# A graph layer with mixing and experts on one core: the change of phases written as one table of steps

## The chip, the cores and the metric

One core of a Trainium2 chip runs the whole program in one launch. TensorE (PE) multiplies matrices, VectorE (DVE), ScalarE (ACT) and GpSimd (POOL) do the rest, and SyncE (SP) issues most DMAs. Each engine works through its own queue in order and waits on semaphores. The metric is the device time of one execution in microseconds; before the change it is 1598.66 us, the median of 3 runs (1596.49 to 1599.17).

## The reference

6250 nodes with 256 features, 100,000 edges sorted by target, 16 relations, all in float32:

```python
xn = layernorm(x)
transformed = einsum('ni,rio->rno', xn, W_rel)          # 16 relations
gnn = segment_sum(transformed[rel, src] * norm, dst)    # 100,000 edges
q, k, v = split(xn @ Wqkv)                              # 8 heads of 32
context = einsum('bnhd,bnhv->bhdv', softmax(k, over nodes), v)
gate = sigmoid(gelu((xn*ln_g + ln_b) @ Wg1 + bg1) @ Wg2 + bg2)
x = x + gnn + ((q @ context) * gate) @ Wproj + bproj
t = layernorm(x)                                        # experts
out = t + sum over the two best of 8 experts e: weight_e * (gelu(t @ w1[e] + b1[e]) @ w2[e] + b2[e])
return x + out
```

## The kernel before

The 6250 nodes lie in 49 row tiles of 128. **The first phase** (to about 720 us) takes tile by tile: it normalises, multiplies with the 16 relation matrices and stores the result as a `table` in HBM (four stores of a quarter each per tile), stores keys and normalised rows (`kv_d`), transposed rows and gate values, and from tile 24 on also gathers and sums the edges whose messages are already in the table. A product of two float32 matrices is made of three products of rounded halves (a high and a low part, `three`, L1826); a product in full float32 ("whole") is one instruction pair of twice the length.

**The second phase** takes pairs of row tiles, `i` = 0 to 23. Each pair has 8 edge groups, `S = 8 i + s`, alternately of three and two tiles of 128 edges: GpSimd gathers the rows of the table (`gathers`, L818, a ring of six groups), ScalarE scales them (`MSGS`), VectorE makes the selection matrix (`SELECT`) and, for split sums, the low part (`MSGS`), TensorE sums (`SUMS`) and VectorE adds the sum to the rows (`adds`). Groups of the pairs below `WHOLE` = 2 (S = 0 to 15) are summed whole, without low parts, the others in split halves. Then a pair goes through the mixer (`OUT`, `GATES`, `GATE`, `PROJ`), its second normalisation (`STATS`, GpSimd's `roots2`, `MEAN`, `NORM`, `TURN`), the choice of experts (`LOGIT`, `TOP`, `COMB`) and eight experts (`LAYER1`, `LOW`, `LAYER2`, `ADD`). In the loop three pairs overlap: the edges of pair i, the mixer of pair i-1, the experts of pair i-2, in the order of `SLOTS_OF_PAIR`, eight slots to a pair.

**Between the phases** the contexts of the mixer have to be finished. The keys of the first 24 tiles have been summed against a first maximum; the last four tiles are still in SBUF (`kvs`); the 21 tiles between come back from `kv_d` in six parts of 4 and 3 (`load_rows`, then `shifts` on VectorE, `exps` on ScalarE, `contexts` on TensorE). SyncE loads them after the last table store, then the first pair's rows (`load_pair`), then the expert weights in four chunks of 2 x 512 KB (`load_chunk(4)` to `(7)`), each of which ScalarE and VectorE split into high and low halves of the whole chunk (`split_hi`, `split_lo`). The later parts of the returned rows (256.5 KB for a tile) lie where the weights of chunks 6 and 7 go, so those two are split after the contexts; the third chunk is loaded when the first is split. GpSimd starts the gathers when the last table store has landed. At that point it also makes the head mask (`heads`, in `ctxbd`).

The order of these steps beside pairs 0 and 1 comes from three places: the tuple `SLOTS_OF_SECOND`, the constants below, and conditions in each engine's `slot_of`:

```python
PARTS_OF_SLOT = {0: (0, 1), 1: (2,), 2: (3,), 3: (4,), 4: (5,)}
SPLITS = ((0, 4), (0, 5), (1, 0), (1, 1))
SPLITS_LOW = ((0, 5), (0, 6), (1, 1), (1, 3))
```

On GpSimd the roots of pair 0 stand before the sixth group of pair 1 (`FIRST_ROOTS`), those of other pairs before the last gather of the next pair (`ROOTS`). VectorE, TensorE and GpSimd have a branch for edges that sum outside their window (`far`), which these inputs don't take.

## Time and profile before

| what | us |
|---|---|
| median of the runs | 1598.66 |
| the profiled execution | 1598.54 |
| its span | 1596.7 |
| PE busy in the span | 1563.8 (98%) |
| DVE busy | 1339.1 (84%) |
| ACT busy | 962.8 (60%) |
| POOL busy | 1021.2 (64%) |

The busy time of an engine is the time in which at least one of its instructions ran; for PE that is generous, since matmuls are pipelined and their ends are modelled. The granted clock is TensorE's, as a share of 2.4 GHz: 1.00 is that level, 0.50 the level of 1.2 GHz. A timeline row has the start, the duration from the first start to the last end of the instructions merged in it, the engine, the line, and in brackets how long the engine had been idle and what released it. SPq is the queue in which SyncE issues DMAs.

### The profile page before, as it was taken

How to read it: one execution, taken by the hardware profiler on the slowest of the kernel's cores; microseconds unless marked ns; L12 is line 12 of the kernel's file. 1: busy time of each engine (PE TensorE's matmuls, PEld its weight loads, DVE VectorE, ACT ScalarE, POOL GpSimd, SP SyncE). 2: the span in 40 equal slices, each digit the busy share in tenths (PEclk: the TensorE clock that was granted, in tenths of full speed). 3: DMA queues.
4: the chain of work that ended last, by engine and by line, in shares of the span. 5: the costliest groups of instructions: out<-in, count | busy, mean ns of one | idle time of the engine just before them, and what ended most of it. 6: DMA issues, size and time to landing. Idle time of an engine off the chain costs nothing.

```text
span 1596.7 us, 31746 instructions
## 1 busy us (share of the span) xinstructions
PE 1563.8 (98%) x10509; PEld 1439.2 (90%) x10509; DVE 1339.1 (84%) x3389; ACT 962.8 (60%) x2156; POOL 1021.2 (64%) x1111
## 2 busy tenths in 40 slices
PE   7999999999999999998799999999999999999998
PEld 6888788888888888887699999999999999999998
DVE  7888656488888888884699999999999999999985
ACT  4455322356565665654677776777677777777764
POOL 4433222677777777757687777777777777767720
PEclk9999999999999999999999999999999999999999
DMA  9776665688888889889433333343333333333320
GB/s 301 264 256 242 243 237 226 231 291 272 277 278 279 283 283 284 277 261 317 144 111 108 116 109 108 112 113 104 103 117 107 110 106 109 112 105 113 107 53 10
DMA packets 127076, 290.50 MB, mean 182 GB/s; under 512 B 21271, under 2 KB 49724, under 8 KB 126914
## 3 DMA queue, kind: packets, MB, share of 16 engines
q1 hardware_dynamic: 86068, 177.19, 30.2%
q0 software_dynamic: 39952, 110.13, 26.3%
q8 instruction: 85, 1.39, 0.4%
q10 hardware_dynamic: 894, 1.16, 0.2%
q14 instruction: 77, 0.63, 0.1%
HBM read 149.49 MB, written 138.90 MB: 181 GB/s over the span
## 4 chain that ended last, share of the span: by engine, by line
PE 94%; DMA 1%; DVE 1%; issue 1%; ACT 1%; POOL 1%; ACTq 0%; SPq 0%; DVEq 0%; POOLq 0%
PE bank L1826 74%; PE bank L2030 4%; PE bank L2031 3%; PE bank L1870 2%; PE bank L1871 2%; PE bank L1982 1%; PE bank L1881 1%; PE bank L2026 1%; POOL raw L700 1%; DMA raw<-table,idxa 1%; PE bank L2068 1%; PE bank L2080 1%; PE bank L1836 1%; DMA pad<-in_L_mix_Wg 1%; PE bank L2077 1%
## 5 line engine op out<-in xcount | busy, mean ns | idle before, releaser
L818 POOL DMA_INDIRECT stg<-table,idxcur x495 | 546.7, 1104 | 145.1 <-issue 133.1
L1826 PE MATMUL bank<-wreg,xt 128*128 128x512 f32 x2352 | 579.1, 397 | 0.2
L1826 PEld LDWEIGHTS bank<-wreg,xt 128*128 128x128 f32 x2352 | 433.4, 189 | 88.0 <-ACT stg L864 1.0
L700 POOL DMA_INDIRECT raw<-table,idxa x297 | 306.6, 1032 | 87.7 <-issue 73.7
L1826 PE MATMUL bank<-tt,wreg 128*128 128x256 f32 (+1 forms) x2400 | 324.4, 284 | 0.0
L1826 PE MATMUL bank<-wreg,ht 128*128 128x256 f32 x2352 | 313.1, 282 | 0.2 <-DVE ht L1727 0.2
L1826 PEld LDWEIGHTS bank<-tt,wreg 128*128 128x128 f32 x2400 | 300.4, 189 | 2.5
L1826 PEld LDWEIGHTS bank<-wreg,ht 128*128 128x128 f32 x2352 | 292.1, 189 | 0.4 <-DVE ht L1727 0.4
L1090 ACT ACTIVATE raw<-bank,cols 128x256 f32<-128x256 f32 (+1 forms) x400 | 164.8, 463 | 101.4 <-PE bank L1826 101.0
L1611 DVE SCALAR_TENSOR_TENSOR ml<-stg,nrm,mh 128x256 fp32r<-128x256 f32 x455 | 195.2, 478 | 13.0 <-ACT mh L1034 13.0
L1034 ACT ACTIVATE mh<-stg,nrm 128x256 fp32r<-128x256 f32 x455 | 200.8, 499 | 0.0
L889 ACT ACTIVATE mh_a<-raw,nrm 128x256 fp32r<-128x256 f32 x297 | 129.6, 500 | 118.1 <-DMA raw<-table,idxa 117.8
L1228 DVE COPY stg<-bank 128x512 f32<-128x512 f32 x196 | 134.2, 686 | 75.5 <-PE bank L1826 74.5
L1741 DVE SCALAR_TENSOR_TENSOR xres<-bank,raw,xres 128x256 f32<-128x256 f32 x392 | 169.7, 473 | 13.1 <-PE bank L1826 11.4
L864 ACT COPY stg<-bank 128x512 f32<-128x512 f32 x196 | 112.5, 581 | 101.8 <-PE bank L1826 100.2
L1361 DVE SCALAR_TENSOR_TENSOR ml_a<-raw,nrm,mh_a 128x256 fp32r<-128x256 f32 x297 | 126.7, 480 | 53.0 <-ACT mh_a L889 52.5
L1095 ACT CAST ht<-raw 128x512 fp32r<-128x512 f32 (+1 forms) x200 | 122.5, 612 | 72.4 <-PE bank L1826 67.4
L1727 DVE TENSOR_TENSOR ht<-raw,ht 128x512 fp32r<-128x512 f32 (+1 forms) x200 | 134.6, 673 | 11.7 <-ACT ht L1095 9.5
L2030 PE MATMUL bank<-mh,sel 128*128 128x256 f32 x455 | 120.3, 291 | 0.0
L2031 PE MATMUL bank<-ml,sel 128*128 128x256 f32 x455 | 117.0, 281 | 0.0
L665 POOL TENSOR_TENSOR xres<-xres,bpb 128x256 f32<-128x256 f32 x24 | 19.4, 809 | 136.0 <-DVE kvs L1215 135.5
L1594 DVE TENSOR_TENSOR sel<-dbl,dpr 128x384 fp32r<-128x384 f32 x198 | 95.0, 480 | 9.7 <-PE bank L2026 9.6
(244 smaller groups left out, 2134.8 us busy)
## 6 DMA issues: line engine op xcount, KB each, us to landing
table<-stg SPq DMA_DIRECT2D x196, 512.0 KB, 3.9
kv_d<-kvs SPq DMA_DIRECT2D x49, 256.5 KB, 5.2
xt_d<-xt SPq DMA_DIRECT2D x49, 256.0 KB, 4.7
xtp<-xt_d SPq DMA_DIRECT2D x24, 512.0 KB
stg<-table,idxcur POOLq DMA_INDIRECT x495
sk<-kv_d SPq DMA_DIRECT2D x24, 256.5 KB, 5.7
out_x<-xres SPq DMA_DIRECT2D x24, 256.0 KB
xres<-in_x POOLq DMA_DIRECT2D x23, 256.0 KB, 4.2
```

The lines of the kernel that those rows point to most:

```text
L700: pool.indirect_dma_start(ring_a[:, r * EARLY + j, :], None, table[0:LIMIT, :], bass.IndirectOffsetOnAxis(ap=idxa[:, at:at + 1], axis=0)). ...
L818: pool.indirect_dma_start(stg[:, ring_at(S, j), :], None, table, bass.IndirectOffsetOnAxis(ap=idxcur[:, at:at + 1], axis=0)).then_inc(gath ...
L889: act.activation(mh_a[:, (r % 2) * EARLY + j, :], ring_a[:, r * EARLY + j, :], ACT.Copy, scale=nrm[:, bass.ds(EB * q + j, 1)]).then_inc(hi ...
L1034: act.activation(mh[:, (s % 2) * CUT + j, :], stg[:, ring_at(S, j), :], ACT.Copy, scale=nrm[:, bass.ds(at + j, 1)]).then_inc(msg_hi, 1)
L1090: act.activation(hf[e % 2][:, c * 256:c * 256 + nt * P], bank[2 + e % 2][:, c * 256:c * 256 + nt * P], ACT.Gelu, bias=b1c[:, 2 * e + c:2 * ...
L1228: dve.tensor_copy(stage[:, j // 2, (j % 2) * 512:(j % 2 + 1) * 512], bank[3 + j % 4][:]).then_inc(copied(k, j)[0], 1)
L1611: dve.scalar_tensor_tensor(out=ml[:, m, :], in0=stg[:, ring_at(S, j), :], scalar=nrm[:, bass.ds(at + j, 1)], in1=halves(mh[:, m, :]), op0= ...
L1727: dve.tensor_tensor(ht[e % 2][:, LO, :, 0:n], cols2(hf[e % 2], n), halves(ht[e % 2][:, HI, :, 0:n]), ALU.subtract).then_inc(h_lo, 1)
L1741: dve.scalar_tensor_tensor(out=xk, in0=bank[6 + e % 2][:, a * C:(a + 1) * C], scalar=comb[:, a, e:e + 1], in1=xk, op0=ALU.mult, op1=ALU.ad ...
L1826: mm = pe.matmul(dst, stat(a, c), mov(b, c), start=(n == 0), stop=(n == 3 * chunks - 1))
L2030: pe.matmul(bank[u % 2][:, 0:C], sel[:, m, :], mh[:, m, :], start=(s % 2 == 0 and j == 0), stop=False)
L2031: mm = pe.matmul(bank[u % 2][:, 0:C], sel[:, m, :], ml[:, m, :], start=False, stop=(s % 2 == 1 and j == PART[1] - 1))
```

## The change

All steps of the pairs 0, 1 and 2 and of the change of phases stand in one tuple, `CHANGE`, in the order in which they are to run; each engine follows it and takes the entries that are its own (`follow`). `run` starts the loop with pair 3. `SLOTS_OF_PAIR` is unchanged but for a new name: the second half of `NORM` is now `KEEP` and stands right behind it. In the table `KEEP` stands later. The other parts:

- SyncE loads five of the returned rows (`FREE_ROWS`) in the last tile, right behind the store of the second quarter of its table rows, instead of behind the last quarter. The shifts and exponentials of the first two parts stand before the branch on far edges.
- TensorE's branch on far edges stands behind the first two parts of rows.
- The whole groups are S = 4 to 19 (`WHOLE_GROUPS`), not 0 to 15.
- The four expert chunks are split in halves (`HIGH n h`, `LOW_PART n h`), most of them behind the contexts; the splits are counted half by half (`splits_of`).
- The head mask is a `[P, 4]` tile made in the setup; the step `HEADS` reads it broadcast.
- The Gelu table is loaded in a step of its own (`GELU_TABLE`), before the contexts.
- The roots of pair 0 stand before the fifth group of pair 1, those of pair 1 before a gather of the sixth group of pair 2 (`EARLIER_ROOTS`). The second copy of indices of pair 0 stands between its gathers.
- Gelu's output and the choice of experts have buffers of their own (`hf`, `mix`), no longer in `raw`.

```diff
-    ROOTS, FIRST_ROOTS = (7, 1), (5, 0)
+    ROOTS, EARLIER_ROOTS = (7, 1), {1: (4, 0), 2: (5, 1)}
+    FREE_ROWS = 5
...
+        hf = [cd[:], wv[:].rearrange("p c n -> p (c n)")]
+        def whole(S):
+            return WHOLE_GROUPS[0] <= S < WHOLE_GROUPS[1]
+        def splits_of(n, h):
+            return 4 + 2 * (n - 4) + h + 1
...
+                    if at(k, NT - 1) and h == 1:
+                        sp.wait_ge(sum_a, ER)
+                        for b2 in range(2):
+                            sp.wait_ge(kv_st[b2], 16 * ((KEPT + SLOTS) // 2))
+                        for n in range(FREE_ROWS):
+                            load_row(n // 4, n)
...
+            sp.wait_ge(ctx1_mm, KEPT)
+            for n in range(FREE_ROWS, SLOTS):
+                load_row(1, n)
             first_phase_over(sp)
...
             for n in range(4, 6):
-                sp.wait_ge(w_lo, n + 1)
+                sp.wait_ge(w_lo, splits_of(n, 1))
                 load_chunk(n + 2)
...
+            def HIGH(n, h):
+                act.wait_ge(raw_in[n % 2], 32 * (n // 2 - 1))
+                if n >= 6:
                     act.wait_ge(ctx_mm, HELD + REST)
+                act.copy(wreg[:, HI, place_of(n), h * CC // 2].rearrange("p r o -> p (r o)"),
+                         raw[:, n % 2, h * WC * C:(h + 1) * WC * C]).then_inc(w_hi, 1)
+            def GELU_TABLE():
+                act.activation(small[0:1, 156:157], small[0:1, 157:158], ACT.Gelu)
             held_exps()
+            for ready in range(2):
+                EXP(ready)
             first_phase_over(act)
...
+            def LOW_PART(n, h):
+                dve.wait_ge(w_hi, splits_of(n, h))
+                dve.tensor_tensor(wreg[:, LO, place_of(n), h * CC // 2].rearrange("p r o -> p (r o)"),
+                                  raw[:, n % 2, h * WC * C:(h + 1) * WC * C],
+                                  halves(wreg[:, HI, place_of(n), h * CC // 2].rearrange("p r o -> p (r o)")),
                                   ALU.subtract).then_inc(w_lo, 1)
...
+            for ready in range(2):
+                SHIFT(ready)
+            dve.wait_ge(flag_ready, 1)
+            far = dve.value_load(flag[0:1, 0:1], min_val=0, max_val=NT * P * R)
+            first_phase_over(dve)
...
+WHOLE_GROUPS = (4, 20)
+CHANGE = (
+    "HELD_ROWS", "ROWS_OF 0", "ROWS_OF 1", "FAR_EDGES", "SELECT 0 0", "SELECT 0 1", "FADE", "SHIFT 2", "EXP 2", "SHIFT 3",
+    "MSGS 0 0", "ROWS_OF 2", "EXP 3", "SUMS 0 0", "ROWS_OF 3", "SHIFT 4", "MSGS 0 1", "EXP 4", "SELECT 0 2",
+    "ROWS_OF 4", "SUMS 0 1", "SHIFT 5", "EXP 5", "SELECT 0 3", "MSGS 0 2", "ADDS 0 0", "ROWS_OF 5", "MSGS 0 3", "GELU_TABLE",
+    "SUMS 0 2", "SUMS 0 3",
+    "CONTEXT", "SELECT 0 4", "MSGS 0 4", "SELECT 0 5", "CONTEXT_PE", "CONTEXT_TURN", "SUMS 0 4", "HIGH 4 0", "MSGS 0 5",
+    "VALUES", "ADDS 0 1", "LOW_PART 4 0", "HEADS", "SUMS 0 5", "HIGH 4 1", "HIGH 5 0", "SELECT 0 6", "QUERY", "GATES 0 2",
+    "LOW_PART 4 1", "QUERY_ROWS", "GATE_ACT 0 2", "OUT 0 2", "MSGS 0 6", "SELECT 0 7", "ADDS 0 2", "SUMS 0 6", "GATE 0 2",
+    "GATE_HI 0 2", "MSGS 0 7", "CLEAR", "GATE_LOW 0 2", "SUMS 0 7", "PROJ 0 2", "HIGH 5 1", "SELECT 1 0", "LOW_PART 5 0",
+    "MSGS 1 0", "ADDS 0 3", "SELECT 1 1", "SUMS 1 0", "LOW_PART 5 1", "MSGS 1 1", "SUMS 1 1", "SELECT 1 2", "ADDS 1 0",
+    "HIGH 6 0", "STATS 0 2", "LOW_PART 6 0", "MSGS 1 2", "SUMS 1 2", "MEAN 0 2", "NORM 0 2", "TURN 0 2", "SELECT 1 3",
+    "TURN_HI 0 2", "TURN_LOW 0 2", "KEEP 0 2", "MSGS 1 3", "SUMS 1 3", "LAYER1 0 2 0", "SELECT 1 4", "HIGH 6 1",
+    "LOGIT 0 2", "LOW_PART 6 1", "LAYER1 0 2 1", "ADDS 1 1", "MSGS 1 4", "TOP 0 2", "LOW 0 2 0", "SUMS 1 4", "HIGH 7 0",
+    "WEIGHT 0 2", "SELECT 1 5", "LOW 0 2 1", "MSGS 1 5", "COMB 0 2", "COMB_HI 0 2", "LAYER1 0 2 2", "LAYER2 0 2 0", "OUT 1 2",
+    "SUMS 1 5", "GATES 1 2", "LOW_PART 7 0", "SELECT 1 6", "ADDS 1 2", "HIGH 7 1",
+    "COMB_LOW 0 2", "ADD 0 2 0", "LOW 0 2 2", "MSGS 1 6", "GATE_ACT 1 2", "GATE 1 2", "LAYER1 0 2 3", "LAYER2 0 2 1",
...
+    "ADD 0 2 6", "LAYER1 1 2 0", "LOGIT 1 2", "SELECT 2 5", "MSGS 2 5", "LAYER2 0 2 7", "LOW 1 2 0", "TOP 1 2", "SUMS 2 5",
+    "LAYER1 1 2 1", "ADDS 2 2", "ADD 0 2 7", "SELECT 2 6", "MSGS 2 6", "SUMS 2 6", "SELECT 2 7", "MSGS 2 7", "SUMS 2 7",
 )
+def follow(order, **steps):
+    for entry in order:
+        name, *numbers = entry.split()
+        if name in steps:
+            steps[name](*map(int, numbers), *((8,) if name in OF_GROUPS else ()))
...
-    for i in range(2, pairs):
+    for i in range(3, pairs):
```

## Rows read from the trace of the kernel before

**Rows 1.** Windows: stretch, length, busy us of each engine (instructions), clock, DMA share, GB/s
```profile
719.88:828.01 108.13, 92.24 (x553) 82.21 (x552) 68.95 (x161) 62.42 (x125) 79.53 (x81) 0.94 0.60 195
767.00:787.30 20.30, 11.30 (x65) 8.87 (x63) 12.03 (x21) 14.03 (x24) 11.74 (x14) 0.98 0.40 118
...
827.63:860.49 32.86, 32.86 (x279) 32.73 (x278) 31.00 (x86) 23.70 (x56) 25.91 (x26) 1.00 0.41 113
...
1484.83:1517.69 32.86, 32.86 (x278) 32.75 (x277) 30.97 (x87) 23.69 (x55) 23.51 (x25) 1.00 0.38 108
```

**Rows 2.** Windows of 2 us in the change of phases, the same columns
```profile
716.00:718.00 2.00, 2.00 (x11) 1.60 (x10) 0.69 (x1) 0.50 (x2) 0.00 (x0) 1.00 0.30 113
...
728.00:730.00 2.00, 0.00 (x0) 0.00 (x0) 0.89 (x1) 1.06 (x1) 1.45 (x2) 0.61 1.08 316
...
786.00:788.00 2.00, 0.66 (x2) 0.60 (x3) 1.18 (x3) 1.97 (x6) 1.53 (x3) 0.62 0.30 76
```

**Rows 3.** Timeline of TensorE at the start and in the change of phases
```profile
12.27 0.29 PE L1801 MATMUL bank<-ident,pad 22*128 22x22 f32 x1 [1.95 <-DMA pad<-in_L_mix_Wg]
...
722.46 3.63 PE L1973 MATMUL bank<-kvs 128*128 128x257 f32 x16
730.03 8.90 PE L1982 MATMUL bank<-slot 128*128 128x257 f32 x28 [3.94 <-ACT slot L996]
...
744.40 1.46 PE L2026 MATMUL bank<-stg,sel 128*128 128x256 f32 x6
...
782.14 1.78 PE L1826 MATMUL bank<-tt,wreg 128*128 128x256 f32 x12
```

**Rows 4.** Waits, 720 to 830 us: who waited for whom, us in total, times, longest
```profile
PE bank L2026 <- ACT stg L1030: 4.1, 2, 2.6
```

**Rows 5.** Timeline of SyncE's queue, around the end of the first phase
```profile
720.92 0.32 SPq L527 DMA_DIRECT2D table<-stg  x1
721.34 3.82 SPq L573 DMA_DIRECT2D slot<-kv_d  x7
```

**Rows 6.** Timeline of GpSimd in the change of phases
```profile
725.00 0.99 POOL L818 DMA_INDIRECT stg<-table,idxcur  x1 [1.23 <-DMA table<-stg]
...
760.60 2.58 POOL L818 DMA_INDIRECT stg<-table,idxcur  x1 [0.30 <-issue]
...
766.12 0.97 POOL L818 DMA_INDIRECT stg<-table,idxcur  x1 [0.16 <-POOL idxcur L740]
...
776.49 0.24 POOL L827 TENSOR_SCALAR small<-small 128x2 f32<-128x2 f32 x1 [5.63 <-DVE small L1666]
```

**Rows 7.** Chain of waits that ended last: start, us, what
```profile
799.39 0.12 PE bank L2030
...
800.58 2.83 PE bank L1826 x24
...
828.01 4.25 PE bank L1826 x36
```

**Rows 8.** Timeline of VectorE in the change of phases
```profile
727.66 1.23 DVE L1540 TENSOR_TENSOR slot<-slot,dg 128x1024 f32<-128x1024 f32 x1 [3.46 <-DMA slot<-kv_d]
...
760.08 2.27 DVE L1186 TENSOR_TENSOR wreg<-raw,wreg 128x2048 fp32r<-128x2048 f32 x1
...
774.31 0.69 DVE L1659 TENSOR_TENSOR xres<-bank,xres 128x512 f32<-128x512 f32 x1
```

**Rows 9.** Timeline of ScalarE in the change of phases
```profile
756.73 1.90 ACT L847 CAST wreg<-raw 128x2048 fp32r<-128x2048 f32 x1 [2.61 <-DMA raw<-in_L_ffn_w]
...
784.00 1.28 ACT L1090 ACT_TABLE_LOAD   x1 [2.39 <-PE bank L1826]
785.29 0.84 ACT L1090 ACTIVATE raw<-bank,cols 128x256 f32<-128x256 f32 x2
786.17 0.62 ACT L1095 CAST ht<-raw 128x512 fp32r<-128x512 f32 x1
786.69 2.10 ACT L1030 ACTIVATE stg<-stg,nrm 128x256 f32<-128x256 f32 x5
```

More of the change, by code:

```diff
@@ L273, in gps_layer @@
         half = small[:, 38:40]
+        heads = small[:, 52:52 + NB]
         vea = small[:, 64:64 + NT - K2]
@@ L797, in _ @@
                     pool.wait_ge(far_x, k + 1)
+            for h in range(PIECES):
+                pool.wait_ge(tbl_st[h], 16 * NT)
             def gathers(i, groups):
```

258 lines of the change are left out of this document (98 added, 160 removed), and 10 rows, old and new, of the table CHANGE.

## The prediction

> **What bounds the kernel now.** I read the windows of the second phase first. From about 828 us on, TensorE is busy for the whole of each stretch of 32.86 us, one pair of row tiles each; the first and last of 21 such rows stand in [rows 1]. So whatever time the change of phases takes is passed on to the end, one for one. The change of phases itself, from the last relation product (719.88) to the start of the loop's fourth pair (828.01), is 108.13 us long, and TensorE is busy in 92.24 of them [rows 1]: 15.89 us idle. That is the first thing to take. The second is the granted clock: it falls to the 1.2 GHz level twice, in the windows 728:730 (0.61 on average) and 786:788 (0.62) [rows 2], each time after TensorE had stood still or nearly so. At that level 28 context products took 8.90 us, where at 0.227 us each (16 in 3.63) they would take 6.35 [rows 3].
>
> What ends the idle time? The timeline names the largest piece: 3.94 us until the first returned key/value rows had been shifted and exponentiated [rows 3]. The waits name the next: 4.1 us for gathered messages that ScalarE had not scaled yet [rows 4]. Then I followed the queues behind these. SyncE issues the first seven rows at 721.34, right after the last table store at 720.92 [rows 5]. GpSimd starts its gathers at 725.00, and issues the last of the twelfth group at 766.12; then it waits 5.63 us, until 776.49, for the statistics of pair 0 [rows 6]. The first expert product starts at 782.14 [rows 3], the fourth at 800.58, the loop at 828.01 [rows 7]. These three moments are the milestones of my sum.
>
> **Rows fetched early.** Five loads leave the place after the last table store and go behind the second quarter's store. SyncE spends 3.82/7 = 0.55 us on each [rows 5], 2.7 us for five; the third and fourth quarter of the last table store and one gate store are queued behind them. The DMA engines are only 0.30 busy in 716:718 [rows 2], and five rows are 5 x 256.5 KB = 1.31 MB, some 4.2 us at the 316 GB/s of window 728:730 [rows 2]. They fit into the gap, so I leave the last table store, and with it the first gather (725.00), where it is; the cost is 0 to 4.2 us, value 0. VectorE is free at 727.66 - 3.46 = 724.20 [rows 8]. Then one shift (1.23) and one exponential (some 1.1, from the shift's end at 728.89 to TensorE's 730.03): the products start at 726.6. TensorE ends the four held tiles at 722.46 + 3.63 = 726.1, so 3.4 of the 3.94 us go, and with them the first fall of the clock (2.5).
>
> **The order by time, up to the contexts.** TensorE now does all returned rows with only four edge groups between them. Its next wait is the third part of rows, behind VectorE's own branch on far edges. That branch lay hidden in VectorE's 3.46 us [rows 8]; it costs between 0 and 3.46, I take 1.0, nearer the lower end, since nothing waits in it. The second shift ends at about 728.6, selections, fade and third shift bring VectorE to 732.6, the exponential to 733.7; TensorE is covered until 732.7 by the first seven rows and loses 1.0. Its own branch, moved to this place, passes within that wait. From 733.7 fourteen rows (four products of 0.217 each, 12.1) and groups one and two in split halves (six and four products of 0.12 [rows 7]) end at 747.0; before, the rows ended at 755.4. Then groups three and four (1.2), the turn of the contexts, a wait for a selection (0.9 together), group five (1.30), values (0.9), group six (0.87), the query product (1.2 with its wait; the small mask has the same 128x128 form) bring TensorE to 753.4, and the query rows, one step each on ScalarE and VectorE, to 754.8: output product of pair 0. With it, groups seven and eight (one wait on ScalarE), the projection, groups nine and ten and two additions, the sums that the statistics need are there at 763.4. Of the halves, one on ScalarE (second chunk) stands ahead of the query rows. Before, ScalarE waited 2.61 us for that chunk, until 756.73 [rows 9]; the queue of loads ahead of it is 1.31 MB shorter, so I put it at 752.5, in time.
>
> **What is late next: GpSimd.** None of this speeds up a gather. They start at 725.00 and go one every 1.25 us, so the twelfth group's last one still ends at 766.12 + 0.97 = 767.1, and 0.4 us later because one index copy now lies between gathers. From the statistics' start to the roots it took 776.49 - 774.31 = 2.2 us [rows 6, 8], so from 763.4 they are there at 765.6, and the walk above may be 2 us too short without a loss. So the roots start behind the twelfth group, at 767.8, where they started at 776.49. From the roots to the first expert product it took 782.14 - 776.49 = 5.65 us, with a sum of three tiles in it (1.30); now it has the two messages of group twelve (0.84), behind ScalarE's second normalising pass, and their last sum (0.43). I take 0.6 more, between -1.3 and +2.3 (nothing hidden): 774.05, 8.1 us earlier.
>
> *The shared port.* The gather of 760.60 took 2.58 us instead of 0.97; it ended 0.83 us after the 2.27 us weight split that VectorE had begun at 760.08 [rows 6, 8]. So a split holds up a gather. Five halves, at most 1.15 us of hold each, now come before the roots in place of two whole splits: between 0 and 5.7 us, against 1.6 for the one in the rows and at most that again for the other. I take no difference, and keep -3 to +3 for the range. The Trainium skill, SBUF — State Buffer, "Who interferes with whom", has it that such an operation (two inputs from SBUF, no two-port mode) takes only the shared read side, and infers that descriptors need the write side. By that no split would delay a gather, and the sum would have no such term; the row disagrees, and I go by the row.
>
> **From the first to the fourth expert product.** Before: 800.58 - 782.14 = 18.4 us. It holds the load of the Gelu table (1.28) [rows 9], which the change puts where ScalarE waits for gathers, and a half-speed stretch. New: three first-layer steps, one second-layer step and an output product at 4.25/3 = 1.42 each [rows 7], logits and gates 0.95, groups thirteen and fourteen 1.30 + 0.87 (six products to the next start: 1.30 [rows 3]): 10.2 us of TensorE. One wait remains: on ScalarE the Gelu pair and cast (0.84 + 0.62), a half split (1.90/2), the next Gelu pair and cast, and then the first two of three messages (0.42 each, 2.10 for five [rows 9]) come before group thirteen ends, 2.4 us after it could. So 12.6 us: the fourth expert product starts at 786.65.
>
> **From there to the loop.** Before: 27.43 us. New: three edge groups more lie behind this point (1.30 + 0.87 + 1.30 = 3.5), and three are now done whole instead of in split halves (0.87, 1.30 and 0.87 against four, six and four products of 0.12: 1.4 more): 32.3 us in all. The whole groups are only moved: sixteen before and after, so the phase's work is the same; VectorE's splits of messages move from the third pair to the first. In these 32.3 us VectorE has 31.4 us of work by my count (its 31.00 of 32.86 in the loop [rows 1], less half of the message splits, plus two half weight splits, two selections and additions), so it is as full as in the loop, no worse. The loop starts at 786.65 + 32.3 = 818.95.
>
> **The clock.** From 761.6 to 774 TensorE works 3.6 of 12.4 us (three groups and a turn), more sparsely than before the second fall (11.30 of 20.30 us [rows 1]). Between nothing and 2.8 us is lost (the span from the first to the second expert product at 1.2 instead of 2.4 GHz); I take 2.0, since the fall before came some way into the expert work. The loop starts at 820.95 and not 828.01: 7.1 us saved.
>
> **At no cost:** the mask moved to the setup (three small GpSimd operations; TensorE then waits 1.95 us for a weight DMA [rows 3], which covers them; up to 1 us if that cover were gone), other buffers for the Gelu output, the roots placed earlier for pairs 1 and 2, the second normalising pass as its own step (in the loop the order is unchanged).
>
> **The sum.** The profiled execution took 1598.54 us, span 1596.7 and 1.84 around it; the median of the runs is 1598.66, no different. 1598.54 - 7.1 = 1591.4 us.
>
> **Rivals.** *The clock holds and the gathers run a little faster* (halves hold them less): 2.0 + 2 more, 1587.4. For: the pauses by my walk are near 3 us each, shorter than the 3.94 before the first fall. Chance 0.23. *The rows don't come early*, because their loads queue among the stores: the start at 730 stays, but GpSimd's pace decides 767 anyhow; 2 us of the gain go, 1593.4. Chance 0.10. *The waits only move*: the second chunk comes at 756.73 as before, so the query rows, queued behind its split on ScalarE, move 4.3 us, the roots 2, and VectorE, full from 786 on, gives away 3 more: 1596.4, within 0.2% (about what a measurement of this kernel can tell from no change). Chance 0.13. *Slower: the last table store is pushed back by the early rows.* Every gather waits for it, so the whole chain from 725.00 moves by as much; from 7.1 us on nothing is gained, and at 11 us the time is 1602.5. For: the rows are larger than that store and ahead of it in one queue. Against: 1.31 MB is 4.2 us, and the engines are idle then. Chance 0.09, 0.07 of it over 0.2%. The forecast itself: 0.45.
>
> So faster 0.45 + 0.23 + 0.10 + 0.03 = 0.81, same 0.12, slower 0.07. Range: down to 13.5 us saved (clock, gathers and ScalarE's wait all well), up to 1 us saved (where the waits move): 1585.0 to 1597.5; outside it some 0.05 and 0.13.
>
> **What would show it.** TensorE's idle time before the first returned rows under 1 us, full clock at 730; the rows' products over by about 747; the first gather at 725 and the roots behind the twelfth group, near 768, with no wait for statistics; the first expert product near 774, the loop near 821. Wrong if the first gather comes late, if the statistics still hold the roots, or if VectorE makes TensorE wait after 786.

## The result, and the profile of the changed kernel

The changed kernel takes 1603.11 us, the median of 9 runs (1601.30 to 1609.18). The kernel before, run beside it 9 times, took 1598.66 (1596.49 to 1600.49). The ratio is 1.0034, with a 95% interval of 1.0022 to 1.0045: slower by 0.34%, some 5.4 us by the ratio (the two medians lie 4.5 us apart). The forecast was 1591.4 us, faster.

Two profiled executions are not laid over each other by their clock times here. The moment at which TensorE starts the products of the four held tiles is 722.46 us in the trace of before [rows 3] and 721.93 in that of after, and in the traces of the experiments it lies anywhere from 717.55 to 725.32, though none of them touches most of the first phase. So all times below are counted from that moment. The marks of before are those of [rows 7] where they stand there, which date the fourth expert product and the loop 0.16 us later than the timeline does; the forecast holds its 2.0 us for the clock in the loop's row alone.

| us after the held tiles' start | before | forecast | after |
|---|---|---|---|
| returned rows' products start | 7.6 | 4.1 | 4.0 |
| first gather starts | 2.5 | 2.5 | 4.6 |
| output product of pair 0 | 43.1 | 32.3 | 37.0 |
| roots of pair 0 | 54.0 | 45.3 | 48.5 |
| first expert product of pair 0 | 59.7 | 51.6 | 56.1 |
| fourth expert product | 78.1 | 64.2 | 70.6 |
| start of the loop | 105.5 | 98.5 | 111.35 |

After leads before by 7.5 us at the fourth expert product, and trails it by 5.8 us at the loop. The loop itself is as before: 32.86 us for a pair, TensorE busy throughout, as in [rows 1]. So what was gained is lost in the last third of the change of phases. Not all of these 13.3 us are a loss: this stretch now holds three edge groups more, and three of its groups are now summed whole, 4.9 us of work by the forecast's count. First the windows of after: the two stretches on either side of the fourth expert product, both together, a loop pair, and 10 us in the rows' part (columns as in [rows 1]).

```profile
721.93:792.54 70.61, 55.53 (x294) 48.01 (x295) 40.22 (x93) 39.94 (x78) 50.93 (x52) 0.93 0.72 236
792.54:833.28 40.74, 34.52 (x248) 32.01 (x247) 28.56 (x73) 24.53 (x57) 29.29 (x30) 0.99 0.36 104
721.93:833.28 111.35, 90.06 (x540) 80.01 (x541) 68.78 (x165) 64.47 (x134) 80.22 (x82) 0.95 0.59 188
840.00:872.86 32.86, 32.86 (x278) 32.75 (x277) 28.98 (x82) 22.30 (x52) 20.75 (x21) 1.00 0.34 95
730.00:740.00 10.00, 6.35 (x22) 4.96 (x21) 3.78 (x7) 3.90 (x7) 7.69 (x10) 0.83 1.01 338
```

In the second stretch TensorE works 34.52 of 40.74 us. Before, the stretch between the same two marks (800.58 to 828.01) had 232 products in place of 248, and TensorE was never idle in it:

```profile
800.58:828.01 27.43, 27.43 (x232) 27.32 (x232) 24.16 (x63) 19.19 (x44) 22.22 (x21) 1.00 0.36 107
```

Neither VectorE (28.56 busy of 40.74) nor any other engine is full in the stretch of after. So it is not an engine's load that holds TensorE; it is a wait in somebody's queue. The timeline of TensorE in after shows where: the rows, then the turns and sums with a wait in front.

```profile
721.93 3.71 PE L1987 MATMUL bank<-kvs 128*128 128x257 f32 x16
725.92 6.33 PE L1996 MATMUL bank<-slot 128*128 128x257 f32 x28 [0.29 <-ACT slot L1005]
735.91 5.42 PE L1996 MATMUL bank<-later 128*128 128x257 f32 x16 [3.65 <-ACT later L1005]
...
758.90 1.65 PE L1842 MATMUL bank<-xtp,wqc 128*128 128x256 f32 x12 [1.02 <-DVE wqc L1796]
...
773.70 0.66 PE L2084 MATMUL bank<-ident,scr 128*128 128x128 f32 x4 [4.49 <-ACT scr L1069]
776.51 2.04 PE L2040 MATMUL bank<-stg,sel 128*128 128x256 f32 x4 [2.15 <-ACT stg L1041]
777.99 3.12 PE L1842 MATMUL bank<-tt,wreg 128*128 128x256 f32 x12
...
816.26 0.66 PE L2084 MATMUL bank<-ident,scr 128*128 128x128 f32 x4 [1.52 <-ACT scr L1069]
820.68 0.36 PE L2044 MATMUL bank<-mh,sel 128*128 128x256 f32 x1 [1.47 <-DVE ml L1629]
825.92 0.36 PE L2044 MATMUL bank<-mh,sel 128*128 128x256 f32 x1 [0.30 <-DVE ml L1629]
830.76 0.35 PE L2044 MATMUL bank<-mh,sel 128*128 128x256 f32 x1 [2.60 <-DVE ml L1629]
832.29 0.56 PE L2044 MATMUL bank<-mh,sel 128*128 128x256 f32 x1 [0.32 <-DVE ml L1629]
```

The first two rows answer to [rows 3]: the wait of 3.94 us is now 0.29, and 28 products take 6.33 us at the full clock instead of 8.90. The wait is back ten microseconds later, at the third part (3.65). The last five rows hold 6.2 us of waits before the loop. The releaser of four of them reads VectorE, which splits the scaled messages and so waits for ScalarE. The timelines of VectorE and ScalarE:

```profile
825.29 0.88 DVE L1629 SCALAR_TENSOR_TENSOR ml<-stg,nrm,mh 128x256 fp32r<-128x256 f32 x2 [2.85 <-ACT mh L1048]
...
829.47 0.54 DVE L1612 TENSOR_TENSOR sel<-dbl,dpr 128x384 fp32r<-128x384 f32 x1
830.13 1.28 DVE L1629 SCALAR_TENSOR_TENSOR ml<-stg,nrm,mh 128x256 fp32r<-128x256 f32 x3
```

```profile
814.59 0.62 ACT L1112 CAST ht<-wv 128x512 fp32r<-128x512 f32 x1 [1.69 <-PE bank L1842]
815.12 1.09 ACT L1069 ACTIVATE scr<-xres,small 128x256 f32<-128x256 f32 x2
...
828.19 0.84 ACT L1107 ACTIVATE wv<-bank,cols 128x256 f32<-128x256 f32 x2 [2.53 <-PE bank L1842]
829.06 0.62 ACT L1112 CAST ht<-wv 128x512 fp32r<-128x512 f32 x1
829.59 2.10 ACT L1048 ACTIVATE mh<-stg,nrm 128x256 fp32r<-128x256 f32 x5
```

ScalarE, at 60% of its time, stands idle 2.53 us for an expert's product from TensorE, then does that expert's Gelu and cast, and only then scales the messages for which TensorE, with nothing else left in its own order, has been waiting. The two engines wait for each other in turn. At the longest wait (2.60, group 2 6) VectorE was no earlier: it made the selection for that group until 830.01 and began to split the first message at 830.13, hardly after ScalarE can have scaled it (five messages in 2.10 us from 829.59). In the same way the normalisation of pair 1 stands behind the eighth expert's cast (814.59), and the turn at 816.26 waits for it.

The first gather answers to the 725.00 of [rows 6], the roots to its 776.49:

```profile
726.55 0.97 POOL L831 DMA_INDIRECT stg<-table,idxcur  x1 [0.97 <-DMA table<-stg]
...
770.43 1.00 POOL L840 TENSOR_SCALAR small<-small 128x2 f32<-128x2 f32 x1 [2.13 <-DVE small L1687]
```

SyncE's queue of after, where the five early rows stand ahead of the last two table quarters and the gate store (compare [rows 5]), and two pieces of the chain of waits:

```profile
714.45 3.68 SPq L559 DMA_DIRECT2D slot<-kv_d  x5
718.23 0.38 SPq L544 DMA_DIRECT2D table<-stg  x1
719.70 0.32 SPq L556 DMA_DIRECT2D hg_d<-hgt  x1
720.62 0.32 SPq L544 DMA_DIRECT2D table<-stg  x1
721.95 1.07 SPq L559 DMA_DIRECT2D slot<-kv_d  x2
724.93 9.46 SPq L559 DMA_DIRECT2D later<-kv_d  x14
```

```profile
719.70 4.97 DMA hg_d<-hgt
...
726.35 7.17 DMA later<-kv_d
```

The gate store takes 4.97 us to land. SyncE may not issue the remaining fourteen rows before it has, and so starts them at 724.93. In e1 below, without the early rows, a copy on GpSimd that waits for the same store starts 2.55 us after its issue (720.48 after 717.93); in after it is 5.69 (725.39 after 719.70).

### The profile page after: what moved, and what is told of

The parts are those of the page before. It is cut to its first block, busy times and chain, and to the rows that moved or that the text cites. A ratio compares the mean times of both kernels' runs of the same rounds, so it can differ in the third digit from the quotient of the medians.

```text
span 1603.2 us, 31756 instructions
## 1 busy us (share of the span) xinstructions
PE 1564.6 (98%) x10509; PEld 1439.0 (90%) x10509; DVE 1338.3 (83%) x3393; ACT 962.9 (60%) x2161; POOL 1031.3 (64%) x1111
## 4 chain that ended last, share of the span: by engine, by line
PE 90%; DMA 3%; POOL 2%; issue 2%; ACT 2%; DVE 1%; SPq 1%; ACTq 0%; POOLq 0%; DVEq 0%
PE bank L1842 71%; PE bank L2044 4%; PE bank L2045 3%; PE bank L1886 2%; POOL raw L723 2%; PE bank L1887 2%; DMA raw<-table,idxa 1%; PE bank L1897 1%; PE bank L2040 1%; PE bank L1996 1%; DMA xres<-in_L_gnn_weight 1%; PE bank L2084 1%; PE bank L2096 1%; PE bank L1852 1%; PE bank L2093 0%
## 5 line engine op out<-in xcount | busy, mean ns | idle before, releaser
L1762 DVE SCALAR_TENSOR_TENSOR xres<-bank,mix,xres 128x256 f32<-128x256 f32 x392 | 169.7, 473 | 18.1 <-PE bank L1842 16.4
L1377 DVE SCALAR_TENSOR_TENSOR ml_a<-raw,nrm,mh_a 128x256 fp32r<-128x256 f32 x297 | 126.3, 479 | 54.8 <-ACT mh_a L898 54.8
L1107 ACT ACTIVATE wv<-bank,cols 128x256 f32<-128x256 f32 (+1 forms) x200 | 82.4, 463 | 62.2 <-PE bank L1842 62.2
L1107 ACT ACTIVATE cd<-bank,cols 128x256 f32<-128x256 f32 (+1 forms) x200 | 82.5, 463 | 46.4 <-PE bank L1842 46.1
L1112 ACT CAST ht<-wv 128x512 fp32r<-128x512 f32 (+1 forms) x100 | 61.2, 612 | 55.7 <-PE bank L1842 53.5
```

Source lines behind the costliest of these rows:

```text
L1107: act.activation(hf[e % 2][:, c * 256:c * 256 + nt * P], bank[2 + e % 2][:, c * 256:c * 256 + nt * P], ACT.Gelu, bias=b1c[:, 2 * e + c:2 * ...
L1377: dve.scalar_tensor_tensor(out=ml_a[:, m + j, :], in0=ring_a[:, r * EARLY + j, :], scalar=nrm[:, bass.ds(EB * q + j, 1)], in1=halves(mh_a[ ...
L1762: dve.scalar_tensor_tensor(out=xk, in0=bank[6 + e % 2][:, a * C:(a + 1) * C], scalar=comb[:, a, e:e + 1], in1=xk, op0=ALU.mult, op1=ALU.ad ...
```

## The experiments

Every experiment was timed in five rounds beside the kernel before, and ratios are to that kernel. The marks are in us after the held tiles' start, from each kernel's profiled execution:

| kernel | first gather | first expert | fourth expert | loop | ratio, 95% interval |
|---|---|---|---|---|---|
| before | 2.5 | 59.7 | 78.1 | 105.5 | 1 |
| after | 4.6 | 56.1 | 70.6 | 111.3 | 1.0034 [1.0022, 1.0045] |
| e1 after, rows late | 2.7 | 57.0 | 71.4 | 112.1 | 1.0051 [1.0032, 1.0070] |
| e2 after, tail mended | 4.6 | 55.2 | 69.2 | 104.9 | 1.0000 [0.9988, 1.0013] |
| e3 after, roots late | 4.5 | 53.9 | 69.1 | 109.5 | 1.0030 [1.0019, 1.0042] |
| e4 before, rows early | 4.7 | 61.0 | 79.8 | 107.2 | 1.0017 [1.0005, 1.0029] |
| e5 e2, rows not held by the gate store | 4.1 | 56.5 | 69.6 | 105.3 | 1.0002 [0.9988, 1.0015] |
| e6 e2, front mended | 4.2 | 51.0 | 64.1 | 99.8 | 0.9959 [0.9945, 0.9973] |
| e7 e5 and e6 | 5.3 | 52.6 | 64.8 | 100.5 | 0.9958 [0.9943, 0.9973] |
| e8 e6, rows late | 2.8 | 56.0 | 67.9 | 103.6 | 0.9966 [0.9953, 0.9979] |
| e9 after, two messages moved | 4.3 | 56.5 | 70.6 | 109.6 | 1.0022 [1.0011, 1.0033] |
| e10 after, normalisation moved | 5.1 | 54.8 | 72.7 | 111.7 | 1.0023 [1.0012, 1.0033] |
| e11 e6, chunk not moved | 4.2 | 53.8 | 68.2 | 103.9 | 0.9974 [0.9963, 0.9985] |
| e12 e2, chunk moved | 4.4 | 55.9 | 70.2 | 105.9 | 0.9987 [0.9975, 1.0000] |

The marks of single executions differ even where nothing was edited. In after, e2, e3, e9 and e10 the order up to the fourth expert product is the same, and the output product of pair 0 lies 33.7 to 37.0 us after the held tiles, the first expert product 53.9 to 56.5, the fourth 69.1 to 72.7. The last stretch, from the fourth expert product to the loop, does not vary like that: with the order of after it is 40.74, 40.73 and 40.37 us (after, e1, e3), with that of e2 35.63 to 35.75 in seven traces (e2, e5 to e8, e11, e12).

**The early rows (e1, e4).** One run takes the early loads out of the changed kernel, one puts them alone into the kernel before.

```diff
 # e1
-                    if at(k, NT - 1) and h == 1:
...
-                        for n in range(FREE_ROWS):
-                            load_row(n // 4, n)
...
             stores(NT - 1, NP, 0)
...
+            for n in range(FREE_ROWS):
+                load_row(n // 4, n)
# e4: the reverse, in the kernel before
```

> The changed kernel, but the five early rows are loaded behind the last table store again, as before the change. Theory A (the early rows delay the stores behind them: the gate store of the last tile took 4.97 us to land, the gathers began at 726.55 in place of 725.00): first gather back at about 725.0, first returned rows' products at about 730, first expert product 0 to 2 us earlier than 778.0, time 0 to 2 us under the changed kernel's. Rival B (the early rows pay, as I had forecast): time 3 to 5 us over the changed kernel's.

> The kernel before with one part of the change alone: five returned rows loaded behind the second quarter's table store. Theory A: first returned rows' products at about 726 in place of 730, but gathers 1 to 1.6 us later, and later returned rows no earlier, so the sums wait instead: time 0 to 2 us over the kernel before. Rival B: 3 to 5 us under it.

In e1 the first gather comes 2.7 us after the held tiles instead of 4.6, so the early rows do push the last table quarter back, by 2 us. But TensorE then waits 4.8 us for the rows (3.94 in the kernel before), and the time does not fall, as theory A had it, nor rise by rival B's 3 to 5 us: 1605.5, ratio 1.0051 against 1.0034, and the intervals overlap. In e4 the same five loads make the kernel before slower by 0.17%: its order has nothing to do with earlier rows, and its gathers come late all the same. The rows are not what makes the changed kernel slow, and no run here shows that they pay.

**The tail (e2, e3).** The entries of the table's last three blocks in a new order, nothing else: the normalisation ahead of the eighth expert's Gelu, its kept copy further back, and the selections and messages of the groups 2 3 to 2 7 further forward, those of 2 5 to 2 7 each ahead of the expert that stood before them.

```diff
-    "ADD 0 2 4", "LOW 0 2 6", "MSGS 2 2", "LAYER1 0 2 7", "SUMS 2 2", "LAYER2 0 2 5", "MEAN 1 2", "NORM 1 2", "KEEP 1 2",
-    "BIAS2 0 2", "SELECT 2 3",
+    "ADD 0 2 4", "LOW 0 2 6", "MSGS 2 2", "SELECT 2 3", "MEAN 1 2", "NORM 1 2", "LAYER1 0 2 7", "SUMS 2 2", "LAYER2 0 2 5",
+    "BIAS2 0 2", "MSGS 2 3",
...
+    "SELECT 2 4", "MSGS 2 4", "ADDS 2 1", "SUMS 2 4", "KEEP 1 2", "SELECT 2 5", "MSGS 2 5",
...
+    "ADD 0 2 6", "LAYER1 1 2 0", "LOGIT 1 2", "SUMS 2 5", "SELECT 2 6", "MSGS 2 6", "LAYER2 0 2 7", "LOW 1 2 0", "TOP 1 2",
+    "ADDS 2 2", "SUMS 2 6", "SELECT 2 7", "MSGS 2 7", "LAYER1 1 2 1", "ADD 0 2 7", "SUMS 2 7",
```

> The changed kernel with another order of the last three groups of steps of the table (pair 2 from its third group on): messages and selections stand ahead of the expert steps whose ScalarE part they were queued behind, the second normalisation of pair 1 ahead of the eighth first-layer step, the second normalising pass behind the turn. Theory C (the loss lies in the order behind the fourth expert product: TensorE waits 6.2 us there for messages queued behind Gelu steps, and its clock falls): loop starts at 825 to 827 and not at 833.5, time 6 to 8 us under the changed kernel's, some 1596. Rival D (GpSimd's 4.28 us wait for the roots of pair 1 makes the last groups' rows late): loop not before 831, time at most 2.5 us under the changed kernel's.

> The changed kernel, but the roots of pair 1 stand before the last gather of pair 2 again, as in the loop. Theory C: the gathers behind come 4 us earlier and nobody waits for them; time within 1 us of the changed kernel's. Rival D: 3 to 5 us under it.

e2 is at 1597.65 us, ratio 1.0000: the order of three blocks is worth 0.34%, the whole of the measured loss, a little less than the 6 to 8 us expected. The window from the fourth expert product to the loop in e2:

```profile
787.53:823.16 35.63, 33.39 (x248) 31.44 (x247) 27.11 (x71) 23.90 (x56) 26.73 (x26) 1.00 0.35 101
```

The same 248 products, 5.1 us sooner: the waits fall from 6.2 to 2.2 us, and the busy time from 34.52 to 33.39. A part of these 1.1 us is the half clock at the end of the stretch of after: 0.50 granted from 832.29 to 833.28, where e2 has 1.00 throughout, which makes 0.5 us at most. In e3 GpSimd no longer stands still for the roots of pair 1 (4.28 us in after), and the stretch is 40.37 us, as long as it was. The ratio is 1.0030. GpSimd's pause was in nobody's way.

**Two parts of the tail, one at a time (e9, e10).** e9 moves the messages and selections of groups 2 5 and 2 6, e10 the normalisation of pair 1. The moves of groups 2 3, 2 4 and 2 7 and of one addition are in neither.

```diff
 # e9
-    "ADD 0 2 6", "LAYER1 1 2 0", "LOGIT 1 2", "SELECT 2 5", "MSGS 2 5", ...
-    "LAYER1 1 2 1", "ADDS 2 2", "ADD 0 2 7", "SELECT 2 6", "MSGS 2 6", "SUMS 2 6",
+    "ADD 0 2 6", "SELECT 2 5", "MSGS 2 5", "LAYER1 1 2 0", "LOGIT 1 2", ...
+    "SELECT 2 6", "MSGS 2 6", "LAYER1 1 2 1", "ADDS 2 2", "ADD 0 2 7", "SUMS 2 6",
 # e10
-    ... "MSGS 2 2", "LAYER1 0 2 7", "SUMS 2 2", "LAYER2 0 2 5", "MEAN 1 2", "NORM 1 2", "KEEP 1 2", ...
-    ... "MSGS 2 4", "SUMS 2 4",
+    ... "MSGS 2 2", "MEAN 1 2", "NORM 1 2", "LAYER1 0 2 7", "SUMS 2 2", "LAYER2 0 2 5", ...
+    ... "MSGS 2 4", "KEEP 1 2", "SUMS 2 4",
```

> The changed kernel (1603.1 us) with two entries moved alone: the messages of groups 2 5 and 2 6 (with their selections) each ahead of the Gelu of the next expert on ScalarE. If TensorE's two waits for them (2.6 us and 0.3 before the loop) are a loss of their own: the wait of 2.6 goes, the way from the fourth expert's product to the loop is 37.5 to 38.5 us instead of 40.8, and the run is 2 to 3.5 us below 1603.1. Rival H (a place on ScalarE given to the messages is taken from the experts: the Gelu that stands behind them comes late, and TensorE waits for that): the sum of its waits between 812 and 834 stays at 5.5 to 6.5 us, and the time stays within 1 us.

> The changed kernel (1603.1 us) with the normalization of pair 1 moved alone: ahead of the eighth expert's Gelu and cast on ScalarE, and its kept copy behind the messages of group 2 4. If the wait of 1.52 us at the turn, and the 1.47 us behind it at group 2 4, come of the place of the normalization alone: both go, the way from the fourth expert's product to the loop is 37.5 to 39 us instead of 40.8, and the run is 1.5 to 3 us below 1603.1. With the part of the messages it makes up the 5.5 us of both together. Rival H: the Gelu comes late instead, the sum of TensorE's waits there stays at 5.5 to 6.5 us, and the time stays within 1 us.

The stretch falls from 40.74 to 38.94 (e9) and 38.99 (e10), 1.8 us each, and the ratios to 1.0022 and 1.0023. That is outside the range expected for e9 (37.5 to 38.5) and at the edge of e10's (37.5 to 39). The waits fall from 6.2 to 5.1 and 4.4 us, below rival H's 5.5 to 6.5, though in e9 not by much, and TensorE nowhere waits for a Gelu that came late. But in e9 a wait does move one place on. TensorE's rows with a wait in this stretch, first e9, then e10:

```profile
813.21 0.66 PE L2084 MATMUL bank<-ident,scr 128*128 128x128 f32 x4 [1.52 <-ACT scr L1069]
817.64 0.35 PE L2044 MATMUL bank<-mh,sel 128*128 128x256 f32 x1 [1.47 <-DVE ml L1629]
827.80 0.36 PE L2044 MATMUL bank<-mh,sel 128*128 128x256 f32 x1 [2.00 <-DVE ml L1629]
```

```profile
817.77 0.36 PE L2044 MATMUL bank<-mh,sel 128*128 128x256 f32 x1 [1.47 <-DVE ml L1629]
823.01 0.35 PE L2044 MATMUL bank<-mh,sel 128*128 128x256 f32 x1 [0.28 <-DVE ml L1629]
827.86 0.36 PE L2044 MATMUL bank<-mh,sel 128*128 128x256 f32 x1 [2.60 <-DVE ml L1629]
```

In e9 the wait of 2.6 at group 2 6 becomes one of 2.0 at group 2 7, the next in line. In e10 the wait at the turn goes, the 1.47 behind it stays, against the expectation. The two parts give 3.6 us together, e2 gives 5.1. Whether the rest comes from the moves that are in neither part, among them group 2 7 where e9's wait went, or only when all are moved at once, no run separates. Nor does one separate the engines: the normalisation (e10) is ScalarE's, but the moves of e9 and e2 bring VectorE's selections forward as well as ScalarE's messages.

**The later rows (e5).** SyncE's wait ahead of the fourteen later rows is cut to what they need; the wait for the gate store goes behind them.

```diff
             for n in range(FREE_ROWS, SLOTS):
                 load_row(1, n)
-            first_phase_over(sp)
+            sp.wait_ge(gnn_mm, 8 * NT)
+            for half in range(2):
+                sp.wait_ge(kv_st[half], 16 * (NP + 1 - half))
             for returned in range(2, 2 * GROUPS):
...
+            first_phase_over(sp)
```

> The kernel with the mended order of the table's last blocks (1597.65 us), and one thing more: the later fourteen rows wait only for the work whose place they take and for their own stores, not for the landing of the last gate store. Theory E (the early rows cost by delaying the gate store and with it the later rows; in the trace of the mended kernel SP issues the first later row at 721.4, 3.1 after the held tiles' products start, and TensorE waits 3.3 us for them): the later rows start about 2 us sooner, TensorE's wait for the third part falls from 3.3 to 1 to 1.5, and the run is 1 to 2.5 us below 1597.65. Rival F (the rows are not what binds there: the chain of gathers is, one each 1.25 us from 722.9 on): the wait for rows falls, but the messages then wait for gathered rows instead, LAYER1 of the first expert stays at 55 us after the held tiles, and the time is within 0.7 us of 1597.65.

The edit is worth nothing: the time is 1597.84 against 1597.65, the ratio 1.0002 against 1.0000. TensorE's wait for the third part is 1.14 us here and 3.31 in e2, and a longer wait stands at the messages of group 1 2:

```profile
769.76 2.90 PE L2043 MATMUL bank<-stg,sel 128*128 128x256 f32 x6 [6.93 <-ACT stg L1044]
```

```profile
769.11 1.31 ACT L1044 ACTIVATE stg<-stg,nrm 128x256 f32<-128x256 f32 x3 [6.19 <-DMA stg<-table,idxcur]
```

The time is as rival F had it. But this one trace doesn't show that the edit shortened the first wait: with this part untouched, the traces of after, e2, e3, e9 and e10 have 3.65, 3.31, 1.87, 0.64 and 1.62 us at the third part, and 0.44, 3.85, 3.89, 6.74 and 3.83 at group 1 2. What they show is a trade: after has the longest wait for the rows and the shortest at group 1 2, e9 the reverse, and their first expert products come at 56.1 and 56.5. A wait saved at the rows can be lost again at the gathered rows. Rival F's reason, the pace of the gathers, is not all of it: in e5 the group's last gather ended at 763.48, and ScalarE waited for its rows for another 5.6 us (the front, below).

**The front (e6, e7, e11, e12).** e6 mends the order between the sums 1 0 and the first Gelu. It holds edits of two kinds. One is for ScalarE: both halves of `HIGH 6` together, `MSGS 1 3` ahead of `KEEP`, `MSGS 1 4` ahead of the first expert's Gelu. The other moves `LOW_PART 5 1` from ahead of the statistics to behind them, and `LOW_PART 6 0` behind the turn. It frees VectorE, and, since SyncE issues the last 1 MB weight chunk and the second pair's rows (0.64 MB) behind `LOW_PART 5 1`, it also puts these loads later. e11 is e6 with `LOW_PART 5 1` left where it was, e12 is e2 with both low parts moved and nothing else; so the move of `LOW_PART 6 0` is in both. e7 is e6 with e5's edit.

```diff
-    ... "SUMS 1 0", "LOW_PART 5 1", "MSGS 1 1", "SUMS 1 1", "SELECT 1 2", "ADDS 1 0",
-    "HIGH 6 0", "STATS 0 2", "LOW_PART 6 0", "MSGS 1 2", "SUMS 1 2", "MEAN 0 2", "NORM 0 2", "TURN 0 2", "SELECT 1 3",
-    "TURN_HI 0 2", "TURN_LOW 0 2", "KEEP 0 2", "MSGS 1 3", "SUMS 1 3", "LAYER1 0 2 0", "SELECT 1 4", "HIGH 6 1",
-    "LOGIT 0 2", "LOW_PART 6 1", "LAYER1 0 2 1", "ADDS 1 1", "MSGS 1 4", ...
+    ... "SUMS 1 0", "MSGS 1 1", "SUMS 1 1", "SELECT 1 2", "ADDS 1 0",
+    "HIGH 6 0", "HIGH 6 1", "STATS 0 2", "LOW_PART 5 1", "MSGS 1 2", "SUMS 1 2", "MEAN 0 2", "NORM 0 2", "SELECT 1 3", "TURN 0 2",
+    "MSGS 1 3", "LOW_PART 6 0", "TURN_HI 0 2", "TURN_LOW 0 2", "KEEP 0 2", "SUMS 1 3", "SELECT 1 4", "MSGS 1 4", "LAYER1 0 2 0",
+    "LOW_PART 6 1", "LOGIT 0 2", "LAYER1 0 2 1", "ADDS 1 1", ...
```

> The kernel with the mended order of the table's last blocks, and its front mended as well: the second half of the sixth weight split's low part goes behind the statistics, both halves of the seventh's high part stand together, the messages of groups 1 3 and 1 4 go ahead of the kept residual and of the first Gelu. Theory G (ScalarE's and VectorE's order around the statistics costs what the forecast of the front missed): TensorE's waits of 2.15 and 2.08 us for messages go, the first expert's product comes 52 to 53.5 us after the held tiles instead of 55.2, and the run is 1.5 to 4 us below 1597.65. Rival F (the chain of gathers binds; its thirtieth gather ends 764.6 in the mended kernel, 46 us after the held tiles): the waits move to the messages of group 1 2 and 1 3, the first expert stays at 54.5 to 55.5, and the time is within 1 us of 1597.65.

> Both mends of the front on top of the mended tail. If E and G both hold and add up: 1593 to 1595, faster than the kernel before by 0.2 to 0.35%. If the chain of gathers binds (rival F): within 1 us of the better of the two alone, since both meet the same gathers; the messages of group 1 2 then wait for gathered rows 3 to 5 us.

> The kernel with the mended tail (ratio to the kernel before 1.0000) and the front's mended order, but with the sixth split's second low part left where the change put it, so that the load of the last weight chunk and of the second pair, which SyncE issues behind that split, start at about 762 us as there. Theory K (in the tail-mended kernel the DMA engines are 0.93 busy from 764 to 770 with these loads, and the gathered rows of group 1 2 land behind them; with the split moved they are 0.32 busy): little of the front's gain of 0.41% is left, the ratio is 0.9985 to 1.0000, and TensorE still waits 4 to 7 us for the messages of group 1 2. Theory G (the order on ScalarE and VectorE is what pays): the ratio is 0.9955 to 0.9975.

> The kernel with the mended tail, and of the front's edit only the low parts of the splits moved: the sixth's second behind the statistics, and the seventh's first behind the next selection, so that the load of the last weight chunk and of the second pair start about 5 us later. Theory K (these loads hold up the gathered rows of group 1 2): the ratio to the kernel before is 0.9955 to 0.9975 (it is 1.0000 without the edit), and TensorE's wait at group 1 2 falls from 3.9 to under 3 us. Theory G: 0.9990 to 1.0000, and the waits of 2.15 and 2.08 us at groups 1 3 and 1 4 stay and carry the loss.

e6 takes 1593.54 us, 0.41% below the kernel before and below e2. Its first expert product comes 51.0 us after the held tiles, outside the 53.9 to 56.5 of the unedited front. e7 is no better (ratio 0.9958, 1592.02 us beside the same runs of before): e5's edit is worth nothing here either, as rival F said. These two are faster than both kernels.

e11 keeps 0.26% of the 0.41, e12 gives 0.13%: 0.39 together, with one small move in both and intervals of some 0.1% to either side. So the order on ScalarE and VectorE (theory G) carries the larger part: e11's ratio lies in G's range and outside K's. e12's lies between the two ranges and proves neither. Theory K's wait of 4 to 7 us for group 1 2 did not come in e11, where TensorE waited 0.96 us, and for VectorE. In e12 that wait was 0.48 us, and 4.45 stood at the turn instead. First e11, then e12:

```profile
763.47 1.53 PE L2040 MATMUL bank<-stg,sel 128*128 128x256 f32 x6 [0.96 <-DVE xres L1643]
```

```profile
764.68 1.53 PE L2040 MATMUL bank<-stg,sel 128*128 128x256 f32 x6 [0.48 <-DVE xres L1643]
770.66 0.95 PE L2084 MATMUL bank<-ident,scr 128*128 128x128 f32 x4 [4.45 <-ACT scr L1069]
```

But this wait in one trace decides nothing, since it ranges from 0.44 to 6.74 us with the loads unmoved. What K rests on can be seen in the windows in which the gathered rows of group 1 2 landed, 764 to 770 us in each of these traces; first e2, then e5, then e6:

```profile
764.00:770.00 6.00, 3.75 (x10) 2.58 (x10) 2.72 (x8) 2.47 (x6) 4.36 (x5) 0.59 0.93 313
```

```profile
764.00:770.00 6.00, 0.24 (x1) 0.27 (x2) 3.26 (x9) 0.89 (x3) 5.22 (x7) 0.77 1.00 335
```

```profile
764.00:770.00 6.00, 3.71 (x22) 2.77 (x20) 3.70 (x9) 4.17 (x8) 4.62 (x7) 1.00 0.32 95
```

With the loads there (0.93 and 1.00 of the DMA engines' time) the messages of group 1 2 start 3.5 and 5.6 us after the end of the last gather issued for them on GpSimd (762.00 and 763.48), with the loads later (0.32) 1.9 us after (768.03). The delay goes with which came first. The last gather of the group and the issue of the second pair's rows, which follows the issue of the weight chunk's first load by 0.96 us; first e5, then e2, then after:

```profile
762.54 0.94 POOL L834 DMA_INDIRECT stg<-table,idxcur  x1 [0.30 <-issue]
762.41 0.51 SPq L604 DMA_DIRECT2D xtp<-xt_d  x1
```

```profile
760.62 1.38 POOL L831 DMA_INDIRECT stg<-table,idxcur  x1 [0.30 <-issue]
762.18 0.51 SPq L601 DMA_DIRECT2D xtp<-xt_d  x1
```

```profile
764.32 0.95 POOL L831 DMA_INDIRECT stg<-table,idxcur  x1 [0.30 <-issue]
767.12 0.51 SPq L601 DMA_DIRECT2D xtp<-xt_d  x1
```

The same two events in all traces with early rows and the new table, counted from the end of the group's last gather:

| traces | the chunk's first load is issued | ScalarE starts on the rows |
|---|---|---|
| e5, e9 | 2.0 us before | 5.6, 5.5 us after |
| e2, e3, e10 | 0.8 before | 3.5, 3.5, 3.5 after |
| after, e11 | 0.9 after | 1.75, 2.3 after (e11 without a wait for rows) |
| e6, e7, e12 | 3.9 to 6.1 after | 1.9, 1.8, 1.8 after |

So the collision is real, and with the order unmoved it is struck or missed by a microsecond or two, from one execution to the next: after and e11 missed it, e2, e3, e9 and e10 did not. What part of e12's 0.13% is the loads and what part VectorE's time ahead of the statistics stays open.

**The early rows once more (e8):** e6 with e1's edit.

> The kernel with both orders mended, front and tail (1593.54 us), but with the five early rows loaded behind the table's last store, as in the first experiment. Theory F (the chain of gathers binds the front: without the 1.28 MB of early rows ahead of it the table's last store lands earlier, and the first gather starts some 2 us sooner after the held tiles, as it did in the first experiment): TensorE waits 4 to 5 us before the rows, as there, but gets it back at the messages of groups 0 5 to 1 3, and the run is 0 to 2 us below 1593.54. Rival A (the early rows pay): the gathers are not what ends last once the order is mended, the wait ahead of the rows stays lost, and the run is 1.5 to 3.5 us above 1593.54.

The ratio is 0.9966, 0.07% over e6's and inside its interval: the 0 to 2 us below e6 of theory F and the 1.5 to 3.5 above of rival A enclose it, and neither is shown. The first gather is 1.5 us sooner than in e6, TensorE waits 4.9 us ahead of the rows, GpSimd then stands idle 4.91 us for the statistics. No change of more than about a microsecond shows, either way.

## Why the prediction was wrong

**The step that failed** is "From there to the loop": 32.3 us from the fourth expert product on, with VectorE "as full as in the loop, no worse". It took 40.74, 8.4 more. Of these, 6.2 are waits, 1.1 is busy time that goes with them (34.52 against 33.39 in e2; half clock in part), and 1.1 is product time that I had priced too low (33.39 against 32.3). I had asked which engine would be full, counted VectorE, and found room. None was full. What held TensorE was the place of entries in the order, ScalarE's above all: before, TensorE waited for no message at all in this stretch; in the new table the messages, the normalisation and the Gelus of one expert after another stand in ScalarE's one queue, and each Gelu waits for TensorE. I did walk ScalarE's queue for group thirteen in the stretch before, where I found the one wait (2.4 forecast, 2.08 measured), and did not walk it here. e2 shows that the order of this stretch is the cause, 5.1 of the 8.4 us, and e10 that ScalarE's place for the normalisation is one part of it. How the waits at groups 2 5 to 2 7 divide between ScalarE's messages and VectorE's selections stays open.

**The front** came 4.5 us late at the first expert product (56.1 against 51.6), and in this execution as much is there at the output product of pair 0 already (37.0 against 32.3): "loses 1.0" for the third part measured 3.65, and the clock fell behind that wait (16 products in 5.42 us where the held tiles' 16 took 3.71, the granted clock 0.83 in 730:740). I had priced the early rows at nothing by looking at the last table store, and had left out the gate store, which the same loads delay and for which SyncE's wait ahead of the later rows stands. But e5 shows that removing this wait is worth nothing, and in the other traces with this front (e2, e3, e9, e10) the wait for the third part is 0.64 to 3.31 us while the first expert product still comes 2.3 to 4.9 us after its forecast. What all five traces have is a wait of 2.15 us for ScalarE's messages of group 1 3 just ahead of the first expert product (776.51 in after): they stand behind the second normalising pass, and from the roots to that product it took 7.6 us and more, where the forecast had 6.25. e6 moves these messages, and the wait is gone. What the front lacks against the forecast is got back by another route, by the order around the statistics (e6: 51.0).

**From the first to the fourth expert product** 14.55 us against 12.6, with the half clock in it (the first product took 3.12 us); the forecast carried 2.0 for the clock as its own term, so that sum was right for this execution. With the same order e2, e3, e9 and e10 took 14.0, 15.3, 14.1 and 17.9.

These make up the whole of the profiled execution: 4.5 + 1.95 + 8.44 - 2.0 = 12.9 us over the forecast's loop start; the held tiles started 0.5 us sooner, and the rest of the run took 769.9 us instead of the 768.7 of before, most of it a half-clock stretch at the loop's start. 1591.4 + 12.9 - 0.5 + 1.2 = 1605.0, as measured there (1605.02).

**What was right:** the rows' start (4.0 after the held tiles against 4.1 forecast), the clock fall at 730 gone (though one came behind the third part, see above), the unchanged loop, and in this execution the clock loss in the experts. **Late next** was not GpSimd: it waited 2.13 us for the statistics, as my last paragraph named as a sign against the forecast, as did the late first gather. A half split still holds a gather: in after the gather of 756.60 took 2.01 us beside the half split that began at 756.57 and took 1.22, so the 0.95 of a gather alone grew by 1.06, near the 1.15 that I allowed. The Trainium skill, SBUF — State Buffer, "Who interferes with whom", infers that such an operation leaves descriptor generation alone; the trace disagrees with this inference here as it did in [rows 6]. The same passage has such an operation contend with GpSimd's reads, which the prediction left out; no run here shows which side it is.

**The rivals.** *The waits only move* was the nearest in kind, but had 3 us in the place where 8.4 were lost. *The last table store pushed back* happened in size 2 us and decides nothing (e1, e8). *The rows don't come early* did not happen. No rival had an order of entries as its mechanism, and the range ended 5.6 us below the median.

## What to carry to other kernels

When work moves from one stretch to another under an order written out by hand, walk the queue of every engine through the new stretch, the half-idle ones first: with no engine full, entries on the wrong side of others that wait for TensorE cost 5 us, and moving some lines of a table gave them back. A wait that ends last is worth only the distance to the one behind it; try its removal alone before counting on it (e5), and look where the wait goes when only a part is moved (e9). Where a load is released by a compute step, moving the step moves the load as well; look at what else wants the DMA engines at that moment.
